# Attention with a row maximum on Trainium2: two-bank row-product tiles, three single-bank score tiles, row fills spread over the tile

## What is computed

```python
x = x + jnp.tanh(g_xattn[0]) * _L0_xattn_ref(_layernorm(x, axis=-1), ctx_1024, ctx_1024, ...)
x = x + jnp.tanh(g_ffn[0]) * _L0_ffn_ref(_layernorm(x, axis=-1), ...)
...
energy = jnp.einsum('mqhd,mkhd->mhqk', q, k) * SCALE
energy = jnp.where(mask == 0, jnp.float32(-1e+20), energy)
attn = jax.nn.softmax(energy, axis=3)
out = jnp.einsum('mhqk,mkhd->mqhd', attn, v)
```

## Time and profile before

| what | value |
|---|---|
| three runs | 8315.55, 8316.77 (median), 8317.08 us |
| profiled execution, its time | 8317.42 us |
| its span | 8315.6 us |
| granted clock, mean over the span | 0.83 of full speed |
| VectorE busy | 6817.8 us (82%) |
| TensorE busy | 5812.3 us (70%) |
| ScalarE busy | 4916.7 us (59%) |
| first and last row fill of the three calls | 203.9 to 8003.5 us |
| first and last exponential of call 1 | 363.4 to 1364.7 us |
| of call 2 | 1741.9 to 2743.4 us |
| of call 3 | 7107.9 to 8109.3 us |

### The profile page before, as it was taken

One profiled execution on the slowest core, in us unless ns is written; L12 is line 12 of the kernel. 1 busy time (PEld: TensorE's weight loads), 2 busy tenths in 40 slices (PEclk: granted clock), 3 DMA queues, 4 the chain that ended last, 5 costly groups with the idle time before them and its releaser, 6 DMA issues. The chain is left out here.

```text
span 8315.6 us, 101743 instructions
## 1 busy us (share of the span) xinstructions
PE 5812.3 (70%) x35301; PEld 1727.6 (21%) x35301; DVE 6817.8 (82%) x14058; ACT 4916.7 (59%) x5921; POOL 754.5 (9%) x394
## 2 busy tenths in 40 slices
PE   5588887568888555543554777767788884788887
PEld 2111112111111111110110111134444441111113
DVE  5999992599996499999997999966665666999953
ACT  3277776147778455543554999954455550677782
POOL 1000000000000000000000000054544450000000
PEclk8699999679999655555556999988988995899998
DMA  7100000300000000000002000000000002000001
GB/s 220 32 2 17 17 1 26 91 3 16 14 4 1 20 8 12 8 8 4 10 7 48 16 14 5 2 29 14 14 9 14 11 4 57 3 16 17 2 1 46
DMA packets 112250, 174.94 MB, mean 21 GB/s; under 512 B 14817, under 2 KB 94726, under 8 KB 106751
## 3 DMA queue, kind: packets, MB, share of 16 engines
q1 hardware_dynamic: 111774, 168.91, 8.0%
HBM read 125.66 MB, written 43.21 MB: 20 GB/s over the span
## 5 line engine op out<-in xcount | busy, mean ns | idle before, releaser
L1028 DVE TENSOR_REDUCE a_partial<-a_row 128x1 f32<-128x494 f32 x4992 | 3024.2, 665 | 169.4 <-PE a_row L908 101.5
L994 ACT ACTIVATE a_prob<-a_score 128x1024 f32<-128x1024 f32 x2448 | 2360.5, 1021 | 608.9 <-PE a_score L921 608.6
L908 PE MATMUL a_row<-a_kg,a_qn 54*128 54x494 bf16 x4992 | 1029.4, 409 | 717.9 <-DVE a_partial L1028 661.7
L933 PE MATMUL a_acc<-a_prob,a_v_all 128*9 128x512 f32 x9792 | 1282.9, 596 | 1.7 <-ACT a_prob L994 1.4
L517 ACT COPY m_rows<-m_score 128x1536 f32<-128x1536 f32 (+1 forms) x640 | 760.8, 1250 | 848.0 <-DVE m_edge L568 672.8
L576 DVE MAX8 m_cand<-m_rows 128x8 f32<-128x192 f32 x4352 | 1213.9, 332 | 13.7 <-ACT m_rows L517 13.7
L496 PE MATMUL m_score<-m_kb,m_qb 54*128 54x512 bf16 (+1 forms) x1664 | 766.1, 608 | 415.8 <-ACT m_rows L517 349.7
L798 DVE SCALAR_TENSOR_TENSOR a_prob<-a_score,a_prob 128x1024 f32<-128x1024 f32 x816 | 924.7, 1209 | 38.9 <-ACT a_prob L774 38.9
L774 ACT ACTIVATE a_prob<-a_score,a_lower 128x1024 f32<-128x1024 f32 x816 | 865.2, 1110 | 86.3 <-PE a_score L715 35.1
L921 PE MATMUL a_score<-a_qb,a_kg 54*128 54x512 bf16 x4896 | 762.5, 380 | 34.7 <-ACT a_prob L994 20.8
L908 PEld LDWEIGHTS a_row<-a_kg,a_qn 54*128 54x128 bf16 x4992 | 243.3, 94 | 2311.8 <-DVE a_partial L1028 2209.8
(11 more groups left out here) (305 smaller groups left out, 5815.0 us busy)
## 6 DMA issues: line engine op xcount, KB each, us to landing
kst<-kv_parts SPq DMA_DIRECT2D x48, 384.0 KB, 3.9
a_kg<-kst SPq DMA_DIRECT2D x60, 306.0 KB
vst<-kv_va SPq DMA_DIRECT2D x48, 288.0 KB, 4.2
e_cb<-comb SPq DMA_DIRECT2D x25, 512.0 KB
a_kg<-kst SPq DMA_DIRECT2D x60, 204.0 KB
a_v_all<-vst SPq DMA_DIRECT2D x3, 3672.0 KB
qst<-q_parts SPq DMA_DIRECT2D x24, 256.0 KB
a_kg<-kst SPq DMA_DIRECT2D x60, 102.0 KB
```

The costliest lines, as they stand in the source:

```text
L908: pe.matmul(row[(use + half) % 3][:, 0:CW], qn[u % 2][rows, pair, i * P:(i + 1) * P], kg[u // NQC % 2][rows, pair, c * CW:(c + 1) * CW], s ...
L933: last = pe.matmul(acc[32 * j:32 * j + VW, :], v_all[:, k, u // NQC * G + j, :], prob[tile % PROBS][:, j // 2, j % 2, :], start=(k == 0), ...
L994: act.activation(prob[tile % PROBS][:, pair, :, :], score[use % 2][:, :, :], ACT.Exp).then_inc(slot_out, 1)
L1028: dve.tensor_reduce(partial[:, u % 2, 2 * item + half, c:c + 1], row[use % 3][:, 0:CW], AX, ALU.max).then_inc(reduced, 1)
```

## The change

The banks are cut the other way. `row` becomes two tiles of two banks, one for a pair of fills: both products raise `filled` once, and VectorE takes both in one reduction of 2 x 494 columns, which gives two maxima. `score` becomes three tiles of one bank: a score pair takes two of the three in turn, each product raises `scored` itself, and ScalarE runs one exponential of 512 columns for each head (and two casts of 512 columns in `keep_queries`). The rule of a score pair is as before, all uses but the last one are read; but a use is now one head, where it was a head pair. The rule of a row pair reads as before too; a use is now a pair.

In TensorE's order the second score pair of a tile now comes at the head of its iteration, ahead of the first fills, and the first score pair of the next tile comes right behind `sums`, ahead of the second fills. Fills and scores thus alternate.

The counts, waits and offsets that follow from this (`bank_use`, `slot_use`, `turn_use`, the waits on `scored` in SyncE's loop and in `place_tops`, the row tile in `heads`) change with it; the places not shown below change in that way alone.

```diff
@@ -827,9 +827,9 @@
-        score = [m.ps(f"score{i}", [P, 2, QC]) for i in range(2)]
+        score = [m.ps(f"score{i}", [P, QC]) for i in range(3)]
         acc = m.ps("acc", [P, QC])
-        row = [m.ps(f"row{i}", [P, QC]) for i in range(3)]
+        row = [m.ps(f"row{i}", [P, 2, QC]) for i in range(2)]
...
@@ -849,15 +849,15 @@
             return 0 if tile < KT + HEADS_AT else (tile - HEADS_AT) // KT
 
         def bank_use(pair_fill, tile):
-            return pair_fill + heads_before(tile)
-
-        def slot_use(tile, pair):
+            return pair_fill // 2 + heads_before(tile)
+
+        def slot_use(tile, j):
 
             u, k = tile // KT, tile % KT
-            return 2 * tile + pair + 1 + u + (1 if k > TURN_AT and u + 1 < UNITS else 0)
+            return G * tile + j + 2 * (1 + u + (1 if k > TURN_AT and u + 1 < UNITS else 0))
 
         def turn_use(u):
-            return 0 if u == 0 else slot_use((u - 1) * KT + TURN_AT, 1) + 1
+            return 0 if u == 0 else slot_use((u - 1) * KT + TURN_AT, G - 1) + 1
 
         @block.sync
         def _(sp):
...
@@ -902,25 +902,24 @@
                     if use >= 2:
                         pe.wait_ge(reduced, use - 1)
                     for half in range(2):
-                        u, item, c = (n + half) // FILLS, (n + half) % FILLS // (2 * NC), (n + half) % (2 * NC) // 2
+                        u, item, c = n // FILLS, n % FILLS // (2 * NC), n % (2 * NC) // 2
                         pair, i = item // QT, item % QT
                         rows = slice(64 * half, 64 * half + ROWS)
-                        pe.matmul(row[(use + half) % 3][:, 0:CW], qn[u % 2][rows, pair, i * P:(i + 1) * P],
-                                  kg[u // NQC % 2][rows, pair, c * CW:(c + 1) * CW], start=True,
-                                  stop=True).then_inc(filled, 1)
+                        last = pe.matmul(row[use % 2][:, half, 0:CW], qn[u % 2][rows, pair, i * P:(i + 1) * P],
+                                         kg[u // NQC % 2][rows, pair, c * CW:(c + 1) * CW], start=True, stop=True)
+                    last.then_inc(filled, 1)
 
             def scores(tile, pair):
                 u, k = tile // KT, tile % KT
-                use = slot_use(tile, pair)
-                if k == 0:
-                    pe.wait_ge(slot_out, turn_use(u) + 1)
+                use = slot_use(tile, 2 * pair)
+                if k == 0 and pair == 0:
+                    pe.wait_ge(slot_out, turn_use(u) + 2)
                 if use >= 2:
                     pe.wait_ge(slot_out, use - 1)
                 for half in range(2):
                     rows = slice(64 * half, 64 * half + ROWS)
-                    last = pe.matmul(score[use % 2][:, half, :], kg[u // NQC % 2][rows, pair, k * P:(k + 1) * P],
-                                     qb[u % 2][rows, pair, :], start=True, stop=True)
-                last.then_inc(scored, 1)
+                    pe.matmul(score[(use + half) % 3][:, :], kg[u // NQC % 2][rows, pair, k * P:(k + 1) * P],
+                              qb[u % 2][rows, pair, :], start=True, stop=True).then_inc(scored, 1)
 
             def sums(tile):
                 u, k = tile // KT, tile % KT
...
@@ -928,7 +927,7 @@
                     pe.wait_ge(v_loaded, 16)
                 if k == 0 and u:
                     pe.wait_ge(ob_ready, u)
-                pe.wait_ge(slot_out, slot_use(tile, 1) + 1)
+                pe.wait_ge(slot_out, slot_use(tile, G - 1) + 1)
                 for j in range(G):
                     last = pe.matmul(acc[32 * j:32 * j + VW, :], v_all[:, k, u // NQC * G + j, :],
                                      prob[tile % PROBS][:, j // 2, j % 2, :], start=(k == 0), stop=(k == KT - 1),
...
@@ -942,43 +941,43 @@
                 if use >= 2:
                     pe.wait_ge(slot_out, use - 1)
                 for pair in range(2):
-                    pe.matmul(score[use % 2][:, pair, :], identb[:, :], qn[u % 2][:, pair, :], start=True, stop=False)
+                    slot = score[(use + pair) % 3]
+                    pe.matmul(slot[:, :], identb[:, :], qn[u % 2][:, pair, :], start=True, stop=False)
                     for i in range(QT):
-                        last = pe.matmul(score[use % 2][:, pair, i * P:(i + 1) * P],
+                        last = pe.matmul(slot[:, i * P:(i + 1) * P],
                                          place[:, pair * QT + i, :, :].rearrange("p s r -> p (s r)"), identb[:, :],
                                          start=False, stop=(i == QT - 1))
-                last.then_inc(scored, 1)
+                    last.then_inc(scored, 1)
 
             def heads(u):
 
                 tile = (u + 1) * KT + HEADS_AT
                 use = bank_use(row_pairs(tile).start if u + 1 < UNITS else UNITS * FILLS, tile) - 1
                 pe.wait_ge(ob_ready, u + 1)
-                pe.wait_ge(reduced, use - 2)
+                pe.wait_ge(reduced, use - 1)
                 for i in range(QT):
-                    last = pe.transpose(row[use % 3][:, i * P:(i + 1) * P], ob[:, i * P:(i + 1) * P], ident[:, :])
+                    last = pe.transpose(row[use % 2][:, 0, i * P:(i + 1) * P], ob[:, i * P:(i + 1) * P], ident[:, :])
                 last.then_inc(filled, 1)
 
             pe.wait_ge(cleared, 5)
             pe.matmul(acc[:, :], zeros[:, 0:P], zeros[:, :], start=True, stop=True).then_inc(acc_zeroed, 1)
             row_fills(-1, row_pairs(-1))
             turn(0)
-            for pair in range(2):
-                scores(0, pair)
+            scores(0, 0)
             for tile in range(UNITS * KT):
                 u, k = tile // KT, tile % KT
+                pairs = row_pairs(tile)
+                scores(tile, 1)
                 if k == TURN_AT and u + 1 < UNITS:
                     turn(u + 1)
                 if k == HEADS_AT and u:
                     heads(u - 1)
-                pairs = row_pairs(tile)
                 row_fills(tile, pairs[:1])
                 if tile:
                     sums(tile - 1)
+                if tile + 1 < UNITS * KT:
+                    scores(tile + 1, 0)
                 row_fills(tile, pairs[1:])
-                if tile + 1 < UNITS * KT:
-                    for pair in range(2):
-                        scores(tile + 1, pair)
             sums(UNITS * KT - 1)
             heads(UNITS - 1)
 
...
@@ -986,19 +985,21 @@
         def _(act):
             def exponentials(tile):
 
-                for pair in range(2):
-                    use = slot_use(tile, pair)
+                for j in range(G):
+                    use = slot_use(tile, j)
                     act.wait_ge(scored, use + 1)
                     if tile >= PROBS:
                         act.wait_ge(summed, tile - PROBS + 1)
-                    act.activation(prob[tile % PROBS][:, pair, :, :], score[use % 2][:, :, :], ACT.Exp).then_inc(slot_out, 1)
+                    act.activation(prob[tile % PROBS][:, j // 2, j % 2, :], score[use % 3][:, :],
+                                   ACT.Exp).then_inc(slot_out, 1)
 
             def keep_queries(u):
                 use = turn_use(u)
-                act.wait_ge(scored, use + 1)
                 if u >= 2:
                     act.wait_ge(summed, (u - 1) * KT)
-                act.copy(qb[u % 2][:, :, :], score[use % 2][:, :, :]).then_inc(slot_out, 1)
+                for pair in range(2):
+                    act.wait_ge(scored, use + pair + 1)
+                    act.copy(qb[u % 2][:, pair, :], score[(use + pair) % 3][:, :]).then_inc(slot_out, 1)
 
             def keep_sums(u):
                 act.wait_ge(summed, (u + 1) * KT)
...
@@ -1021,14 +1022,13 @@
         def _(dve):
             def search(tile):
                 for n in row_pairs(tile):
-                    for half in range(2):
-                        u, item, c = (n + half) // FILLS, (n + half) % FILLS // (2 * NC), (n + half) % (2 * NC) // 2
-                        use = bank_use(n, tile) + half
-                        dve.wait_ge(filled, use + 1)
-                        dve.tensor_reduce(partial[:, u % 2, 2 * item + half, c:c + 1], row[use % 3][:, 0:CW], AX,
-                                          ALU.max).then_inc(reduced, 1)
+                    u, item, c = n // FILLS, n % FILLS // (2 * NC), n % (2 * NC) // 2
+                    use = bank_use(n, tile)
+                    dve.wait_ge(filled, use + 1)
+                    dve.tensor_reduce(partial[:, u % 2, 2 * item:2 * item + 2, c], row[use % 2][:, :, 0:CW], AX,
+                                      ALU.max).then_inc(reduced, 1)
                     if (n + 2) % FILLS == 0:
-                        place_tops(n // FILLS, bank_use(n, tile) + 2)
+                        place_tops(u, use + 1)
 
             def place_tops(u, uses):
 
```

More of the change, by code:

```diff
@@ L881, in _ @@
             for u in range(UNITS - 2):
-                sp.wait_ge(scored, turn_use(u) + 1)
+                sp.wait_ge(scored, turn_use(u) + 2)
                 load_queries(u + 2)
```

(6 more changed lines are left out.)

## The result

The changed kernel takes 8432.69 us (median of four runs, 8430.62 to 8436.01), the kernel before 8316.92 in the same comparison: a ratio of 1.014, interval 1.0122 to 1.0157. It is slower, by 116 us. The profiled execution took 8430.62 us, its span is 8428.8.

What follows compares the result with a forecast made beforehand. VectorE was taken to bound lead and mixed tiles, ScalarE the tail. Per call -26.9 (lead) + 32.6 (mixed tiles) + 27.3 (tail) = +33.0 us; three calls, +99, gave 8416 us from 8317.4, range 8345 to 8490.

Steps and rivals of the forecast that it cites:

- What bounds it: Kernel before: VectorE busy 194.12 of 200 us in mixed tiles and pacing the lead; ScalarE busy all 80 in the tail.
- The cheaper reduction: VectorE's 988-column reduction: 1.17 us long, step 1.12 where two steps were 1.21; lead gains 26.9 us a call.
- the bound of 1.21 to 1.22: Wide reduction not cheaper because each bank costs its own fixed part; 8459 us, counted within the main case's 0.81.
- The link B to A: From a tile's first score pair through its first exponential to its second pair: at least 1.06 us.
- TensorE's part: Mixed tiles, from a tile's second score pair through fill and sums to the next tile's first pair: 1.50 us.
- The tail: Tiles after the last fills: 2.36 us each for 1.86, 27.3 us a call lost.
- What comes on top: Extras in mixed tiles for three-pair tiles, turns, `place_tops` and `heads`: 26.1 us a call.
- A turn: Six mixed tiles a call with a turn's products between the score pairs: 3.33 us for 1.50, 11.0 in all.
- A third pair: 12 mixed tiles with three fill pairs delay TensorE by 0.6 us each, 7.2 a call.
- VectorE as the bound: Rival: mixed tiles need 2.24 us or less, set by VectorE; faster, 8011 us, chance 0.08.
- The even case: Rival: loss and gain cancel at 2.48 us a tile; 8300 to 8334 us, chance 0.05.
- the case drawn from the Trainium skill: Rival: TensorE's clock falls to half in the tail, 3.64 us a tile; 8626 us, chance 0.06.

Runs made afterwards that it cites:

- the last version: Changed kernel with all fills between a tile's two score pairs, five score banks in the tail, waits by head: 8163.14 us, ratio 0.9811 to the kernel before.

## Why the prediction was right, point by point

- **What bounds it.** Before: VectorE in lead and mixed tiles, ScalarE in the tail. With narrow exponentials and four banks the mixed tiles kept their pace and the tail followed ScalarE's step, which bears this out. In the changed kernel, halving VectorE's work moved the mixed tiles by 5 us a call, and halving ScalarE's columns mixed tiles and tail together by 85: neither engine's whole work bounds the mixed tiles now, the one exponential in the loop does, as forecast.
- **The cheaper reduction.** 1.178 us long, for 1.17 from the slope; the bound of 1.21 to 1.22 (a fixed part for each bank) is refuted. The step was 1.094 where I had 1.12: two of these instructions overlap by 0.084, and I had taken 0.05, where the narrow ones show 0.06 and the earlier trace rows 0.08 for wide ones. The lead gained 30.6 for 26.9.
- **The link B to A.** Priced 1.06, measured 1.08, part by part: product to exponential 0.43 for 0.42, exponential 0.594 for 0.597, its end to the next product 0.06 for 0.05. TensorE's part was 1.50, as written. The tile is 2.582 for 2.56, and 0.022 x 353 x 3 is 23 us. Most of it is rounding: the terms named add up to 1.067 and 1.51, not to 1.06 and 1.50, and these 0.017 a tile are 18 of the 23 us.
- **The tail.** 2.37 for 2.36 a tile, 27.7 lost for 27.3.
- **What comes on top.** 937.55 - 353 x 2.582 = 26.1, the very sum, but that is partly luck, since the entries differ. They can be read from the starts of the tiles' exponentials in call 1:

```profile
458.81 2.16 ACT L993 ACTIVATE a_prob<-a_score 128x512 f32<-128x512 f32 x4 [0.42 <-PE a_score L921]
...
463.31 2.16 ACT L993 ACTIVATE a_prob<-a_score 128x512 f32<-128x512 f32 x4 [0.97 <-PE a_score L921]
...
468.48 2.16 ACT L993 ACTIVATE a_prob<-a_score 128x512 f32<-128x512 f32 x4 [0.42 <-PE a_score L921]
...
471.85 2.17 ACT L993 ACTIVATE a_prob<-a_score 128x512 f32<-128x512 f32 x4
474.44 2.16 ACT L993 ACTIVATE a_prob<-a_score 128x512 f32<-128x512 f32 x4 [0.42 <-PE a_score L921]
477.71 2.16 ACT L993 ACTIVATE a_prob<-a_score 128x512 f32<-128x512 f32 x4 [1.11 <-PE a_score L921]
```

  A turn makes a tile 4.50 us (458.81 to 463.31), 1.92 over an ordinary one: 11.5 for 11.0. A third pair costs 0.60, and 13 tiles have one, not 12 (the last mixed tile has a single pair): 7.8 for 7.2. The step of 3.37 from 468.48 is a third pair and the copy, 0.19, and that of 3.27 from 474.44 is `heads`, 0.69: six of both are 5.3 for 5.2. `place_tops` cost nothing, for 2.7. And tile 1 of the call took 4.07 us, 1.5 that I had not listed.
- **The range** of 8345 to 8490 held the 8433. In the profiled execution the sum was 14 us low: 23 of the link and 1 of the tail, against 11 that the lead did better in three calls.
- **The rivals.** VectorE as the bound wanted a link of 0.74, and none in the changed kernel was under 1.07. The even case wanted 0.98. The clock stayed at its full 2.4 GHz through all three tails, with TensorE busy 63.94 of 90 us in the window above, so the case drawn from the Trainium skill, "TensorE: Matmul & The Clock Gate", section "A second HAM failure mode: psum-queue depth-cycling", did not come, as layer 2's row had said. The Trainium skill, "VectorE: DVE Perf Modes", section "The TRN2 errata", says of the latency of SBUF that one large tile pays it once; for reads of PSUM, which these are, its table has a fixed 120 cycles. For VectorE the trace agrees in kind: the same maxima cost 196 us less, and the estimate of 1.15 us by that table was 0.02 short of the 1.178 measured. It says nothing about who waits for whom, and there the time went.

The one reading that did not hold was made after the result: that three full banks could cover the sums. I had counted ScalarE's work and not the bank that the last product before the sums needs.

## What to carry to other kernels

Count the buffers against the products between two long blocks on the producer's queue. With one buffer fewer than products, one consumer's step and two handovers stood in series with the block in every order tried, and what was saved on an engine outside that loop became idle time; here a bank moved from the scores to the maxima cost more than the wider reduction saved. Then move everything that is not in the loop into its waiting half (fills between B and A, 186 us) and lend idle buffers where a phase leaves them free (68 us).

## What was not expected of the hardware

In the tail of the last version, where ScalarE has no gap, the recorded duration of a 512-column exponential grew from 0.59 us up to 1.02 while the steps between starts stayed at 0.49. The exponentials that read a row bank show it (least, median and most, in ns):

```profile
L1004 ACT ACTIVATE a_prob<-a_row x88: 592/995/1019, 1207.7 to 1313.6; 128x512 f32<-128x512 f32 x88
```

The tail with four score banks had no gap either, and the same step of 0.49, but durations of at most 0.70:

```profile
L994 ACT ACTIVATE a_prob<-a_score x169: 668/681/695, 1289.5 to 1371.8; 128x512 f32<-128x512 f32 x169
```

So an engine without gaps does not by itself give 1.02, and what the rest is, a wait inside the engine perhaps, no run here shows. Either way the pace of an engine without gaps has to be read from starts.
